# A selective scan and its projections on one core: first dt tile ahead of B/C, other pairs for the splits, the last out-projection four pairs later, b_out on TensorE

## The reference, cut to what matters

```python
xz = x @ W_in + b_in
x_proj, z = jnp.split(xz, 2, axis=-1)
x_conv = silu(x_proj)                        # "u" in the kernel
A = -jnp.exp(A_log)
x_dbl = x_conv @ W_xproj + b_xproj           # "bc" in the kernel
B, C = jnp.split(x_dbl, 2, axis=-1)
dt = jax.nn.softplus(x_conv @ W_dt + b_dt)
def step(h, xs):
    u_t, dt_t, B_t, C_t = xs
    dA = jnp.exp(dt_t[..., None] * A)
    dBu = (dt_t * u_t)[..., None] * B_t[:, None, :]
    h = h * dA + dBu
    y_t = jnp.einsum('bds,bs->bd', h, C_t) + D * u_t
    return (h, y_t)
y = selective_scan(x_conv, dt, A, B, C, D_param) * silu(z)
return y @ W_out + b_out                     # x = _layernorm(x + this)
```

## Time and profile before

| | us |
|---|---|
| median of 3 runs (3187.53 to 3192.28) | 3189.76 |
| the profiled execution | 3192.79 |
| its span, first to last instruction | 3191.1 |
| DVE busy, whole span (84%) | 2687.3 |
| PE busy (89%) | 2836.6 |
| POOL busy (58%) | 1836.3 |
| ACT busy (63%) | 2016.4 |

### The profile page before, as it was taken

How to read it: one execution, slowest core, us unless ns; L and a number is a source line. 1 busy time by engine, 2 the same in 40 slices (tenths; PEclk the granted TensorE clock), 3 DMA queues, 4 the chain that set the end, 5 groups by cost and what they waited for, 6 DMA issues and landing times. The chain is left out here.

```text
span 3191.1 us, 48817 instructions
## 1 busy us (share of the span) xinstructions
PE 2836.6 (89%) x18964; PEld 1271.5 (40%) x18964; DVE 2687.3 (84%) x3064; ACT 2016.4 (63%) x3618; POOL 1836.3 (58%) x949
## 2 busy tenths in 40 slices
PE   5888988978988988988978889889999999999998
PEld 2222222222222222222222222556666676667765
DVE  3899999999999999999999988666666677777775
ACT  4676776776766766676676745555555555555564
POOL 3698987887887987988988898221111211112100
PEclk8999999999999999999999989899999999999999
DMA  4111111111111111112112143701111000001000
GB/s 154 44 45 55 47 57 43 47 57 44 57 50 50 47 50 60 50 37 65 45 44 83 40 131 125 233 14 48 47 45 41 29 29 22 22 24 34 29 8 14
DMA packets 120118, 172.77 MB, mean 54 GB/s; under 512 B 13265, under 2 KB 48721, under 8 KB 119378
## 3 DMA queue, kind: packets, MB, share of 16 engines
q1 hardware_dynamic: 119890, 169.63, 16.5%
HBM read 100.92 MB, written 66.58 MB: 52 GB/s over the span
## 5 line engine op out<-in xcount | busy, mean ns | idle before, releaser
L790 POOL TENSOR_TENSOR h<-h,c_rep 128x1024 f32<-128x1024 f32 x511 | 1197.2, 2357 | 274.6 <-ACT carry L572 273.8
L719 DVE TENSOR_TENSOR_SCAN h<-r_ps,carry,h 128x512 f32<-128x512 f32 x768 | 938.9, 1262 | 8.8 <-ACT r_ps L566 8.5
L566 ACT ACTIVATE r_ps<-r_ps,decay 128x512 f32<-128x512 f32 x1024 | 632.0, 656 | 357.0 <-PE r_ps L340 356.7
L706 DVE TENSOR_TENSOR h<-u_ps,b_rep 128x1024 f32<-128x1024 f32 x512 | 614.4, 1200 | 64.8 <-PE u_ps L351 63.1
L351 PE MATMUL u_ps<-dtu,spread 32*128 32x512 f16 x2048 | 320.5, 391 | 104.2 <-DVE h L706 103.6
L340 PE MATMUL r_ps<-dt,spread 32*128 32x512 f16 x2048 | 314.7, 387 | 57.4 <-DVE h L719 44.7
L367 PE MATMUL y_ps<-h,gather 128*32 128x512 f32 x2048 | 287.0, 628 | 57.4 <-POOL h L790 54.5
L1824 POOL TENSOR_TENSOR o_in<-o_in,rows 128x1024 f32<-128x1024 f32 x15 | 35.9, 2395 | 510.2 <-DMA o_in<-o_dram 510.2
L719 DVE TENSOR_TENSOR_SCAN h<-r_ps,zero,h 128x512 f32<-128x512 f32 x256 | 313.1, 1264 | 7.9 <-ACT r_ps L566 7.8
L40 PE MATMUL fps<-x,region 128*128 128x256 f16 x1024 | 284.1, 277 | 3.5 <-issue 2.4
L41 PE MATMUL fps<-x,region 128*128 128x256 f16 x1024 | 283.5, 277 | 0.0
(11 more groups left out here) (247 smaller groups left out, 5732.1 us busy)
## 6 DMA issues: line engine op xcount, KB each, us to landing
u_t_dram<-u SPq DMA_DIRECT2D x16, 1024.0 KB, 4.8
z_t_dram<-zs SPq DMA_DIRECT2D x32, 512.0 KB, 3.0
uz<-u_t_dram SPq DMA_DIRECT2D x64, 256.0 KB, 3.9
uz<-z_t_dram SPq DMA_DIRECT2D x64, 256.0 KB, 4.3
y_t_dram<-y SPq DMA_DIRECT2D x64, 256.0 KB, 2.4
region<-y_t_dram SPq DMA_DIRECT2D x32, 256.0 KB, 3.6
result<-x SPq DMA_DIRECT2D x16, 512.0 KB, 2.8
x_t<-dram_x_t SPq DMA_DIRECT2D x15, 512.0 KB, 4.0
```

Of the source, the lines that this page charges most:

```text
L566: nc.scalar.activation(bank, bank, ACT.Exp, scale=decay[:, col:col + 1]).then_inc(s_da, 1)
L706: nc.vector.tensor_tensor(h[:, g % H_GROUPS, o:o + 2, :], u_ps[:, :, :], b_rep[:, c % 2:c % 2 + 1, :].broadcast_to([P, 2, TS]), ALU.mult). ...
L719: nc.vector.tensor_tensor_scan(row, r_ps[:, 2 * (pair % 2) + o, :], row, start, ALU.mult, ALU.add)\
L790: nc.gpsimd.tensor_tensor(rows, rows, c_rep[:, c % 2:c % 2 + 1, :].broadcast_to([P, 2, TS]), ALU.mult)\
```

## The change

In the start, the projection of dt0 stands in front of bc, both in two halves of k, so that the first halves need only the low part of u's first half; they go to two banks of `r_ps`. Of dt1 only the first half stands in the start; its second half is at pair 0. dt0's add, multiplication and low halves are done by DVE, no longer by POOL. The weights of z are split earlier (first half) and inside the loop (second half, behind the scans of pair 0). u and z reloads get semaphores of their own, so that ACT's D*u waits for u alone and DVE's gate for z.

```diff
-            self.order = [f"u{t}" for t in range(8)] + ["bc", "B", "C", "dt0", "dt1", "z0", "z1", "dt2", "z2", "z3", "dt3",
+            self.order = [f"u{t}" for t in range(8)] + ["dt0", "bc", "B", "C", "dt1", "z0", "z1", "dt2", "z2", "dt3", "z3",
...
-            self.z = ((0,), (1,), (5,), (6,), (10,), (11,), (12, 13), (14, 15))
+            self.z = ((1, 2), (3, 4), (8, 9), (13,), (14,), (15,), (19,), (20,))
...
-            self.dt = ((-9,), (-9,), (2, 3, 4), (7, 8, 9), (16, 17, 18), (19, 20, 21), (22, 23, 24), (25, 26, 27))
+            self.dt = ((-9,), (0,), (5, 6, 7), (10, 11, 12), (16, 17, 18), (21, 22, 23), (24, 25, 26), (27, 28, 29))
...
+            d = 2 if n == 1 else 0
+            self.x, self.u_high = (21, 24) if n <= 2 else (19, 23), (36 + d, 44 + d)
...
+    def high_at(self, t):
+        return self.dt[t][-1] + (2 if t < 2 else 3)
```

```diff
             def rep_dtu(pair):
                 c, j, p = place(pair)
+                if p == 0:
+                    pe.wait_ge(s_dlo, c * NJ + j + 1)
...
                 if s in plan.bc:
-                    pe.wait_ge(s_ul, 2 * n + 2)
+                    pe.wait_ge(s_ul, 2 * n + 1 + min(plan.bc.index(s), 1))
...
-            pe.wait_ge(s_ul, 2)
-            pe.wait_ge(s_wl, 3)
-            project(first, "bc", w_xp, 0, u16, 0, NJ, NJ, y_ps[0:2 * NSTATE, :], 2 * NSTATE)
-            pe.wait_ge(s_wl, 4)
-            for t in range(2):
-                if t == 0:
-                    pe.wait_ge(s_const, 8)
-                    for w in range(2):
-                        spread_state(first, w, u_ps[:, w, :])
-                project(first, f"dt{t}", w_dt, t * P, u16, 0, NJ, NJ, pj[:, :])
+            pe.wait_ge(s_ul, 1)
+            pe.wait_ge(s_wl, 4)
+            project(first, "dt0", w_dt, 0, u16, 0, half, NJ, dt0_ps, free=1)
+            project(first, "bc", w_xp, 0, u16, 0, half, NJ, bc_ps, 2 * NSTATE, free=2)
+            pe.wait_ge(s_ul, 2)
+            project(first, "dt0", w_dt, 0, u16, half, NJ, NJ, dt0_ps)
+            project(first, "bc", w_xp, 0, u16, half, NJ, NJ, bc_ps, 2 * NSTATE)
+            project(first, "dt1", w_dt, P, u16, 0, half, NJ, pj[:, :], free=NJ)
+            pe.wait_ge(s_const, 8)
+            for w in range(2):
+                spread_state(first, w, r_ps[:, 2 + w, :])
             rep_dt(0)
             rep_dtu(0)
```

```diff
-W_OUT_AT, OUT_AT = 18, 28
-X0_AT = 38
+W_OUT_AT, OUT_AT = 18, 32
+W_OUT_LOW_AT = (20, 21, 23, 25, 27, 29, 30, 31)
...
                 if part == 1:
+                    if i < 2:
+                        if i == 0:
+                            pe.wait_ge(s_first, 32)
+                            pe.wait_ge(s_fb, 1)
+                        last = nc.tensor.matmul(pj[:, :], x_t[0:1, 1, 0:P], x_t[0:1, 0, :], start=False, stop=True)
                     last.then_inc(s_op, 1)
...
+            def x0_tile(i):
+                dve.wait_ge(s_op, i + 1)
+                if i == 0:
+                    dve.wait_ge(s_first, 32)
+                nc.vector.scalar_tensor_tensor(a["x0"][:, i, :], pj[:, :], UNSCALE, a["x0"][:, i, :], ALU.mult, ALU.add)\
+                    .then_inc(s_oe, 1)
...
+                if s == OUT_AT + 1:
+                    x0_tile(0)
+                if s == OUT_AT + 3:
+                    x0_tile(1)
...
-                if s == X0_AT:
-                    pool.wait_ge(s_first, 32)
-                    pool.wait_ge(s_oe, 2)
-                    nc.gpsimd.tensor_tensor(a["x0"], a["x0"], a["o0"], ALU.add).then_inc(s_fb, 1)
-                if s == X0_AT + 4:
-                    pool.wait_ge(s_fb, 1)
-                    nc.gpsimd.tensor_tensor(a["x0"], a["x0"], x_t[:, 0:1, :].broadcast_to([P, 2, D]), ALU.add)\
-                        .then_inc(a["s_x0"], 1)
```

More of the change, by code:

```diff
@@ L242, in _, with first_steps @@
             next_x(1, 0)
+            def first_steps():
+                sp.wait_ge(s_wl, 7)
+                load_u(0, 0)
+                store_z(0, 0)
+                load_z(0, 0)
+                load_u(0, 1)
+                load_z(0, 1)
+                store_z(0, 1)
+                store_y(0)
+                load_u(0, 2)
+                load_z(0, 2)
+                store_z(0, 2)
+                store_y(1)
+                store_z(0, 3)
+                next_x(1, 1)
+                load_u(0, 3)
+                load_z(0, 3)
+                store_y(2)
             def step(c, j):
                 more = c + 1 < NC
-                if c == 0 and j == 0:
-                    store_z(0, 0)
-                    sp.wait_ge(s_wl, 7)
                 if j == 6 and more:
                     store_z(c + 1, 0)
-                load_uz(c, j)
-                if c == 0 and j == 0:
-                    store_z(0, 1)
-                if j == 0 and 0 < c and more:
+                load_u(c, j)
+                load_z(c, j)
+                if j == 0 and more:
                     next_x(c + 1, 0)
@@ L420, in out_piece @@
                     last = split_product(nc, pj[:, :], [y16[s][:, i % 4, part, tokens] for s in range(2)],
-                                         [w_out[s][:, k, :] for s in range(2)], k == 0, k == NJ - 1)
+                                         [w_out[s][:, k, :] for s in range(2)], k == 0, k == NJ - 1 and i >= 2)
                 if part == 1:
+                    if i < 2:
[3 more added lines that the diff above has]
+                        last = nc.tensor.matmul(pj[:, :], x_t[0:1, 1, 0:P], x_t[0:1, 0, :], start=False, stop=True)
                     last.then_inc(s_op, 1)
@@ L608, in after_exps @@
                         softplus(plan, t)
-                    if s == plan.dt[t][-1] + 2:
+                    if s == plan.high_at(t) and not (n == 0 and t == 0):
                         dt_high(plan, t)
@@ L648, in _ @@
             nc.scalar.activation(decay[:, :], decay[:, :], ACT.Exp).then_inc(s_decay, 1)
-            for part in range(2):
-                for t in range(4 * part, 4 * part + 4):
-                    act.wait_ge(s_pj, t + 1)
-                    src = r_ps[:, t, :] if t < 4 else u_ps[:, t - 4, :] if t < 6 else y_ps[:, :] if t == 6 else pj[:, :]
-                    nc.scalar.activation(u[:, t, :], src, ACT.Silu, bias=b_in[:, t:t + 1], scale=UNSCALE)\
-                        .then_inc(s_ev, 1)
-                u_high(0, part)
-                weights_high(2 + part)
-            load_tables()
-            evacuate_bc(first, y_ps[0:2 * NSTATE, :])
-            evacuate_b(first, u_ps[:, 0, :])
-            evacuate_c(first, u_ps[:, 1, :])
-            for t in range(2):
-                evacuate_dt(first, t)
-                softplus(first, t)
-            weights_high(4)
-            for t in range(2):
-                dt_high(first, t)
-            weights_high(5)
+            for t in range(4):
+                evacuate_first_u(t)
+            u_high(0, 0)
+            weights_high(2)
+            for t in range(4, 7):
+                evacuate_first_u(t)
+            weights_high(4)
+            evacuate_first_u(7)
+            u_high(0, 1)
+            weights_high(3)
+            load_tables()
+            evacuate_dt(first, 0, r_ps[:, 0, :])
+            softplus(first, 0)
+            evacuate_bc(first, r_ps[0:2 * NSTATE, 1, :])
+            dt_high(first, 0)
+            evacuate_b(first, r_ps[:, 2, :])
+            evacuate_c(first, r_ps[:, 3, :])
             act.wait_ge(s_decay, 2)
@@ L735, in _ @@
             weights_low(pieces[2][2], pieces[2][0], pieces[2][3], 3)
+            weights_low(pieces[4][2], pieces[4][0], pieces[4][3], 4)
             dve.wait_ge(s_uh, 2)
+            dve.wait_ge(s_ul, 1)
             nc.vector.tensor_tensor(u16[1][:, 4:8, :], u[:, 4:8, :], u16[0][:, 4:8, :], ALU.subtract).then_inc(s_ul, 1)
-            for n in range(3, 6):
-                weights_low(pieces[n][2], pieces[n][0], pieces[n][3], n + 1)
+            weights_low(pieces[3][2], pieces[3][0], pieces[3][3], 5)
+            dve.wait_ge(s_soft, 1)
+            nc.vector.tensor_tensor(dt[:, 0, :], dt[:, 0, :], soft[:, 0, :], ALU.add).then_inc(s_dt, 1)
+            dve.wait_ge(s_dt, 1)
+            nc.vector.tensor_tensor(soft[:, 0, :], dt[:, 0, :], u[:, 0, :], ALU.mult).then_inc(s_dtu, 1)
+            dve.wait_ge(s_dhi, 1)
+            nc.vector.tensor_tensor(dt16[:, 1, 0, :], dt[:, 0, :], dt16[:, 0, 0, :], ALU.subtract)
+            nc.vector.tensor_tensor(dtu16[:, 1, 0, :], soft[:, 0, :], dtu16[:, 0, 0, :], ALU.subtract).then_inc(s_dlo, 1)
             dve.wait_ge(s_const, 1)
@@ L834, in _ @@
             nc.gpsimd.memset(gather[:, :, :], 1.0).then_inc(s_const, 1)
-            for t in range(2):
-                dt_and_dtu(first, t)
-            for t in range(2):
-                dt_low(first, t)
             pool.wait_ge(s_const, 9)
```

111 lines of the change are left out of this document (67 added, 44 removed).

## The result

The changed kernel takes 3166.09 us (median of 4 runs, 3165.89 to 3167.36) against 3188.98; the ratio is 0.9928, with a 95% interval of 0.991 to 0.9945. So 22.9 us were gained where 51 were forecast, and the time lies outside the range that was given.

A forecast was written before the change was run, and what follows sets the result against it. DVE was taken to bound the scan, so an edit there is worth DVE's idle time. Terms -25 - 8 - 16 - 2 = -51 us took the median 3189.8 to 3139 us; range 3118 to 3160 for 8 in 10.

The forecast's parts named there:

- The start: Before the scan: spreading of dt begins 27 us earlier, pair 2 starts at 62.9 or 63.0 against 87.82; -25 us.
- Chunk 0: First chunk after its first pairs: queue waits go, 7 of 15.5 us of waits left standing; -8 us.
- The 3.92 at pair 8: Chunk 0: DVE's longest wait, 3.92 us, from D*u queued behind the reload of z; claimed to go.
- Chunks 1 to 6: Middle chunks: the wait at pair 51 goes and a little at pairs 30 to 32; -16 us, ends 0 and -37.8.
- The step on the bc edit: Pair 51 of the middle chunks: bc's first third needs only u's first half, so the wait goes; 13.7 us.
- Moving ACT's halves one pair takes the first away ... I count 0.4 a chunk: Pairs 30 to 32, middle chunks: 1.14 us wait goes, POOL stays late; 0.4 us a chunk gained, 2.4 in all.
- The wait at 56 stays: Pair 56 of the middle chunks: DVE's wait of 1.2 us was to remain as it was.
- Last chunk: Last chunk: less waiting for the first `y_low`, x0 moved off POOL; -2 us, ends -12 and +8.
- In all about 6: Last chunk: DVE does x0's two tiles, 0.7 us each, and stands for PE's tile each time; about 6 us.
- (1): Rival: only the start pays, the scan's waits are moved, bc stalls a pair later; -28, 3162 us, chance 0.17.
- (3): Rival: PE drops to 1.2 GHz in the scan, pairs take 5.7 us instead of 3.49; slower, 3205 us, chance 0.03.
- The signs: Expected in traces: pair 2 at 62 to 64 us, chunk 0 waits about 7, none at pair 51, clock not under 0.9.

The follow-up runs named there:

- e11: Changed kernel with dt0's addition, product and low halves given back to POOL; DVE's third multiplication starts at 63.7 us, against 61.3 to 62.5 in the others.
- e12: Changed kernel in which PE begins dt0 and bc only when both low halves of u are made; DVE's third multiplication starts at 68.0 us.
- e5: Changed kernel with chunk 0's z4 at pairs 14 and 15, z5 at 16, and dt4 at 17 and 18; 3157.3 us, ratio 0.9894.
- e17: Changed kernel with dt's high halves and x's split at their old pairs in chunks 2 to 7, the bc edit kept; 3152.7 us, ratio 0.9883.
- e1: Changed kernel with the old pairs for dt's high halves and x's split, and the old bc wait, back in the middle chunks; 3168.7 us, ratio 0.993.
- e8: Changed kernel with extra matmuls ahead of the spreads of B and C, every u tile, and at pairs 22, 26 and 27; 3162.5 us.
- e3: Changed kernel with 6 extra, unread matmuls ahead of each spread of B and C in chunks 1 to 7; 3161.6 us, ratio 0.9915.

## Why the prediction was wrong, step by step

- **The start**, -25: right, -26.5. e11 and e12 confirm two of its terms, DVE for POOL (about 2 us) and the halves (6 us).
- **Chunk 0**, -8: measured +1.4. I had seen the burst of z at pairs 13 to 15 and priced it by matmuls (2.6 us a pair beside 1.4 of other work). What it costs is the wait for a buffer: two rows of `zs` that must be stored first, behind a silu of 3.6 us. The 3.92 at pair 8 did vanish; 8.3 at 17 to 19 took its place (e5 gives back most of it).
- **Chunks 1 to 6**, -16: measured -3.3. The step on the bc edit was right when taken alone: 13.7 forecast, 13.6 measured (e17 against e1). That it fits to the tenth is luck: in e1 the waits at pairs 50 to 52 come to 11.8 us, and the rest of the 13.6 lies elsewhere. The step that failed is "Moving ACT's halves one pair takes the first away ... I count 0.4 a chunk": the moved splits were put at -2.4 us and measured at +12 to +15. I looked for their effect at pairs 30 to 32, where pairs 19 to 34 did get a little shorter, and not behind them. "The wait at 56 stays" was the other error: it came to 13.6 us for 7.2. There was no line for TensorE's clock in this sum at all, though the rows of the kernel before showed both of its levels; I had it only as a rival that would slow the whole scan, and gave that 0.03. In fact it falls for a few us at a time, in both kernels, and decides over the waits at pairs 39 to 43 and at 56 (e8 and e3); the one at 32 is POOL's.
- **Last chunk**, -2: measured +1.3. "In all about 6" for the two x0 tiles was 11.7. The load of x0 behind SP's 23 us of standing (1.98) and the first tile at 1.2 GHz were not in it.
- **The rivals.** (1), only the start pays, gave 3162 and is the nearest, with a chance of 0.17. Its reason in chunk 0 was right, the one in the middle was not: bc does not stall a pair later. (3) had the right resource with the wrong size: the granted clock over the scan is 0.96, where it was 0.95 before.
- The range, 3118 to 3160, ended below (1)'s own 3162. The terms of the scan rested on waits that go when their cause goes, with little set down for those that take their place.
- **The signs** that were named all came out on the forecast's side but one (15.9 us of waits in chunk 0 for 7): no wait at pair 51, a clock over 0.9. They looked at the waits that were to go, and none asked for new waits at pairs 34 to 56, where the forecast failed.
